# Reordering a hand-written queue: SyncE's copies of late key/query sets and first maxima, and TensorE's row blocks behind a tile preparation

## The chip, the cores and the metric

The kernel runs on one core of one Trainium2 chip. The metric is the device time of one execution in microseconds. The core has a matrix engine (TensorE, PE in the profile, with its weight loads as PEld), VectorE (DVE), ScalarE (ACT), GpSimd (POOL), and SyncE (SP), which in this kernel issues every DMA.

## The reference

A block on x of 8 sequences of 1024 tokens of 256 numbers: a layer norm, and then the sum of x, an attention with 16 query heads over 8 key/value heads and linear distance biases (ALiBi), and a linear layer with weights of 8 bits and inputs rounded to 8 bits per token.

```python
xn = _layernorm(x)
q = (xn @ Wq.T).reshape(n, s, 16, 16)
k = repeat((xn @ Wk.T).reshape(n, s, 8, 16), 2, axis=2)
v = repeat((xn @ Wv.T).reshape(n, s, 8, 16), 2, axis=2)
energy = einsum('nqhd,nkhd->nhqk', q, k) - abs(t_q - t_k) * slope_h
attn = softmax(energy / 4, axis=-1)
attention = einsum('nhqk,nkhd->nqhd', attn, v).reshape(n, s, 256) @ Wo.T + bo
x_scale = maximum(max(abs(xn), axis=-1), 1e-6) / 127
x_q = clip(round(xn / x_scale), -128, 127)
linear = (x_q @ weight_q.T) * x_scale * weight_scale + bias
out = x + attention + linear
```

## The kernel before

The work is 64 **units**, one for each batch and key/value head (u = 8 * batch + head), each with two query heads (e = 0, 1), and 64 **tiles** of 128 tokens. Each engine runs its own list of instructions, written out by hand; semaphores tie the lists together. Nothing is reordered at run time, so an instruction that waits holds up all behind it on its engine.

**A unit on PE** (`unit` under `pe`, L1417) has eight slots, c = 0 to 7, one for each block of 128 keys. A slot holds four column products (`col_half`, L1279: scores of a key block against 512 queries of one head, into a ring of three PSUM banks), two row blocks (`ahead_row_block`), and one product with V (`pv_block`, L1355). The column products give the scores that ACT turns into probabilities (L1171). The **row blocks** are scores of 128 queries against all 1024 keys, computed one or two units ahead: row blocks 0 to 7 of unit u are those of unit u + 1, head 1, and 8 to 15 those of unit u + 2, head 0. DVE finds the maximum of each row (L999, "reduction" below). Two PSUM buffers, `ps_row`, take turns, so row block i waits for the reduction of row block i - 2. The maxima go back into the query rows as two extra rows, so that the column products come out less their maximum.

**A row block** comes in two shapes. `half_row_block` (L1296 and L1298) runs two products side by side in the two halves of PE's rows; its second half reads a copy of keys and queries on other partitions, `k_again` and `q_again`. `row_block` (L1279 into `ps_row`) runs eight products in strips of 32 columns and needs no copy.

**Preparation of tiles.** In the odd units 1 to 53, at the end of slot c = 1, PE makes queries, keys, values and the linear layer of one or two tiles (`outputs`, `qkv_whole`, L1395 to L1415) and, from unit 9 on, the output projection of earlier tiles. DVE has its share of that at the same place: normalisation and statistics (L915 to L957), and before them the transposition of the last unit's sums (L1039). A "pair" below is an odd unit from this place on and the even one behind it, up to the next odd unit's preparation.

**SP's list** (`unit` under `sp`, L597) issues, for each unit, the next x tile, the transposed x tile (`load_xt`), the set of keys and queries of unit u + 3 (`next_set`, some 12 DMAs), stores of attention sums and of prepared parts, the token scales (`load_token`, L568), the maxima of unit u + 1 into its query rows (`place_max`, L506, four small DMAs), the attention rows to project (L525), the copy `k_again`/`q_again` of unit u + 3 (`load_again`, L497 and L499) and the outputs. The first column product of a unit waits for its maxima (`set_loaded` up to `WHOLE_SET`).

A set is **late** (`late_set`) when the last tile of its batch is prepared in the very unit that should load it: units 8, 16, ... 56, seven in all. Such a set is loaded at the end of unit u - 3, and its `load_again` comes in unit u - 2, at the end of that unit's list. PE runs the late unit's head 0 as strips, without the copy, in unit u - 2, and its head 1 with the copy from slot 0 of unit u - 1 on (`wait_again`). `load_again(u)` itself waits until the set has landed and until the row blocks of unit u - 2 are done, since the two copies take turns. The change of unit 22 to unit 23 (late set 24) stands for the seven below.

Before the first unit, SP stores the first tiles' parts, loads sets 0 to 2 and the remaining constants, and ends with the first `load_token`, two `load_again` and `place_max(0, 0)`.

Of the kernel before, what the change touches and what calls it, by code (L numbers as in the profile page):

```python
# [41 lines left out]
UNITS = BATCH * KV_HEADS  # L42
# [42 lines left out]
SETS = 4  # L85
# [19 lines left out]
def last_tile(u):  # L105

    return BLOCKS * (u // KV_HEADS + 1) - 1


def late_set(u):  # L110

    return u >= SETS - 1 and last_tile(u) >= PREP_AHEAD and made_unit(last_tile(u)) == u - SETS + 1
# [77 lines left out]
def build(nc, x, x_t, wqk_t, wv_t, wo_t, wo_last_t, w8_t, w_scale, bias_attn, bias_lin, q_alibi, k_alibi, diag,  # L190
          eye, parts_dram, token_dram, att_dram, out):
    ctx = ExitStack()
    with ctx:
# [237 lines left out]
        def _(sp):  # L431
# [20 lines left out]
            def load_set(u, slot):  # L452

                g, tok = u % KV_HEADS, (u // KV_HEADS) * SEQ

                def rows(dst, chunk, row, pick, loaded=set_loaded[slot]):
                    for at, q_parts, k_parts in PAIRS:
                        use = q_parts if pick == "q" else k_parts
                        n = len(use)
                        cols = bass.ds(chunk * TOKENS + tok, SEQ)  # L460
                        here = dst[at:at + n * HEAD_DIM, :]
                        if len(set(use)) == 1:
                            src = parts_dram[bass.ds(row, HEAD_DIM), use[0]:use[0] + 1, cols]
                            sp.dma_start(here, src.rearrange("d j n -> j d n").broadcast_to(  # L464
                                [n, HEAD_DIM, SEQ])).then_inc(loaded, 16)
                        elif list(use) == sorted(use):
                            src = parts_dram[bass.ds(row, HEAD_DIM), use[0]:use[0] + n, cols]
                            sp.dma_start(here, src.rearrange("d j n -> j d n")).then_inc(loaded, 16)
                        else:
                            for j, part in enumerate(use):  # L470
                                src = parts_dram[bass.ds(row, HEAD_DIM), part:part + 1, cols]
                                sp.dma_start(here[j * HEAD_DIM:(j + 1) * HEAD_DIM, :],
                                             src.rearrange("d j n -> (d j) n")).then_inc(loaded, 16)

                pairs = KV_HEADS // (QK_CHUNKS - 1)
                rows(k_set[:, slot, :], QK_CHUNKS - 1, g * HEAD_DIM, "k",
                     first_rows_loaded if u == 0 else set_loaded[slot])
                for e in range(GROUP):
                    rows(q_set[:, slot, e, :], g // pairs, (g % pairs * GROUP + e) * HEAD_DIM, "q",
                         first_rows_loaded if u == 0 and e == 0 else set_loaded[slot])  # L480
                if u >= SETS - 1:
                    load_alibi(u, slot)
# [75 lines left out]
            def store_token(t):  # L558
                sp.wait_ge(xscale_ready, 3 * (t - PREP_AHEAD + 1))
                sp.dma_start(token_dram[t, :, :],  # L560
                             token_of(t)).then_inc(token_stored[t % 2], 16)

            def load_token(t):

                sp.wait_ge(token_stored[t % 2], stored_tokens(t))
                if t >= PREP_AHEAD + 2:
                    sp.wait_ge(xt_scaled, t - 2 - PREP_AHEAD + 1)
                sp.dma_start(token_b[:, t % 2, :, :].rearrange("p n j -> p (n j)"),  # L568
                             token_dram[t:t + 1, :, :].rearrange("a n j -> a (n j)").broadcast_to(
                                 [P, TOKEN * P])).then_inc(token_loaded[t % 2], 16)  # L570
# [15 lines left out]
            for dst, src in ((wscale, w_scale), (bias, bias_attn), (bias2, bias_lin)):  # L586
                sp.dma_start(dst[:, :], src.unsqueeze(0).broadcast_to([P, EMBED])).then_inc(
                    consts_loaded, 16)
            load_set(2, 2)
            sp.dma_start(wo[:, :, :], wo_t.rearrange("(c p) n -> p c n", p=P)).then_inc(  # L590
                consts_loaded, 16)
            sp.dma_start(wo_last[:, :, :], wo_last_t).then_inc(wo_last_loaded, 16)
            for t in (PREP_AHEAD, PREP_AHEAD + 1):
                load_xt(t)
            store_token(PREP_AHEAD)
            load_token(PREP_AHEAD)
            load_again(1, 1)  # L597
            load_again(2, 2)
            place_max(0, 0)

            def unit(u, f):
                if f["next_x"]:
                    next_x(u + X_AHEAD)
                if f["xt"]:
                    load_xt(u + 2 + PREP_AHEAD)
                if f["row_set"] and not late_set(u + 3):
                    next_set(u + 3)
                if u % PAIR == 1:
                    store_att(u - 1)
                for t in f["normed"]:  # L610
                    store_token(t)
                for t in f["made"]:
                    store_parts(t, t % 2)
                if u == UNITS - 3:
                    load_att_last(0, P, UNITS - KV_HEADS // EC)
                if f["last"]:
                    load_att_last(1, P - GROUP * HEAD_DIM, UNITS - 1)
                if f["token"]:
                    load_token(u + 1 + PREP_AHEAD)
                if not f["last"]:  # L620
                    place_max(u + 1, (u + 1) % SETS)
                if f["prev"] and u % PAIR == 0:
                    store_att(u - 1)
                for t in f["next_att"]:
                    load_att_t(t, t % 2)
                if f["row_set"]:
                    if late_set(u + 3):
                        next_set(u + 3)
                    else:
                        load_again(u + 3, (u + 3) % SETS)  # L630
                if u + 2 < UNITS and late_set(u + 2):
                    load_again(u + 2, (u + 2) % SETS)
                for t in finished(u):
                    store_out(t, t % 2)

# [580 lines left out]
        def _(pe):  # L1216
# [202 lines left out]
            def unit(u, f):  # L1419
                for c in range(BLOCKS):  # L1420
                    if c == 0:
                        pe.wait_ge(set_loaded[u % SETS], set_count(u, u % SETS, WHOLE_SET))
                    col_half(u, c, 0, 0)
                    col_half(u, c, 0, 1)
                    ahead_row_block(u, f, 2 * c)
                    ahead_row_block(u, f, 2 * c + 1)
                    col_half(u, c, 1, 0)
                    if c >= 2:
                        pv_block(u, u % 2, c - 2)
                    elif f["prev"]:  # L1430
                        pv_block(u - 1, (u - 1) % 2, BLOCKS - 2 + c)
                    col_half(u, c, 1, 1)
                    if c == 1:
                        for t in f["proj"] or f["made"]:
                            outputs(u, f, t % PAIR)
                        for t in f["made"]:
                            qkv_whole(u, t)
# [52 lines left out]
```

## Time and profile before

| what | value |
|---|---|
| median of 3 runs | 1608.16 us (1606.62 to 1609.25) |
| profiled execution, own time | 1606.43 us |
| its span, first to last instruction | 1604.5 us |
| PE busy | 1507.3 us, 94% of the span |
| DVE busy | 1394.1 us, 87% |
| ACT busy | 1183.8 us, 74% |
| POOL busy | 1073.4 us, 67% |
| mean granted TensorE clock | 0.978 |

The profile is one execution. "Busy" is time in which an engine has at least one instruction in flight. In the timeline, times count from the first instruction; a row can merge several instructions of one kind (x8), and a bracket at its end gives the idle time ahead of it and what ended that. Matmuls overlap: a row of eight column products starts eight matmuls, and the next row may start before the last has drained. The list of waits sums, for each pair of a waiting line and what it waited for, the idle time, how often, and the longest.

### The profile page before, as it was taken

What the parts mean: (1) busy time and instruction counts of PE and PEld (TensorE: products, weight loads), DVE (VectorE), ACT (ScalarE), POOL (GpSimd) and SP (SyncE); (2) the same over time, 40 slices, a digit from 0 to 9 for tenths busy, and PEclk for the clock granted to TensorE, in tenths of its full rate; (3) what the DMA queues carried; (4) which work ended last, traced back from release to release, by engine and by line L of the source; (5) the groups of instructions that cost most, each with busy time, mean ns of one, the idle gap of its engine ahead of it and who ended that gap; (6) DMA issues with size and microseconds to landing.
All of it is one profiled execution on the core that took longest, in us unless ns stands there. A gap on an engine that the chain in (4) does not pass through costs nothing.

```text
span 1604.5 us, 42517 instructions
## 1 busy us (share of the span) xinstructions
PE 1507.3 (94%) x16284; PEld 584.2 (36%) x16284; DVE 1394.1 (87%) x1698; ACT 1183.8 (74%) x2331; POOL 1073.4 (67%) x1627
## 2 busy tenths in 40 slices
PE   5789989999899998999989999899998999899999
PEld 5323323333333333333333334333333333233333
DVE  6889989999799997999979999799987988899991
ACT  3467777777687775887757887677776777688885
POOL 6457877777688875787757787577785776433332
PEclk9899999999999999999999999999999999999999
DMA  6423233343324333333333333333333332212211
GB/s 169 130 62 84 71 99 79 89 98 84 105 72 106 96 79 98 93 93 101 84 84 95 103 90 90 89 94 97 94 86 85 95 85 69 80 44 70 70 42 61
DMA packets 197291, 140.98 MB, mean 88 GB/s; under 512 B 107040, under 2 KB 165728, under 8 KB 197088
## 3 DMA queue, kind: packets, MB, share of 16 engines
q1 hardware_dynamic: 197088, 138.27, 33.0%
q8 instruction: 129, 2.11, 0.6%
q14 instruction: 74, 0.61, 0.1%
HBM read 81.40 MB, written 35.63 MB: 73 GB/s over the span
## 4 chain that ended last, share of the span: by engine, by line
PE 53%; DVE 31%; issue 8%; SPq 4%; DMA 3%; POOL 0%; ACT 0%; POOLq 0%; ACTq 0%
DVE row_max L999 29%; PE ps_ring L1279 17%; PE ps_pv L1355 15%; PE ps_row L1296 11%; PE ps_ring L1395 4%; PE ps_ring L1415 3%; DMA q_again<-q 2%; PE ps_ring L1398 1%; DVE pv_turned L1039 1%; PE ps_row L1279 1%; PE ps_ring L1409 1%; SPq L497 1%; PE ps_row L1387 1%; SPq L464 0%; DMA base<-x 0%
## 5 line engine op out<-in xcount | busy, mean ns | idle before, releaser
L999 DVE TENSOR_REDUCE row_max<-ps_row 128x1 f32<-128x1024 f32 x1024 | 1199.2, 1213 | 153.8 <-PE ps_row L1298 138.5
L1171 ACT ACTIVATE probs<-ps_ring 128x512 f32<-128x512 f32 x2048 | 1083.7, 601 | 284.8 <-PE ps_ring L1279 282.3
L1279 PE MATMUL ps_ring<-q,k 122*32 122x512 bf16 x8192 | 639.2, 385 | 5.6 <-DMA q<-neg_max_t 4.7
L762 POOL TENSOR_TENSOR probs<-probs,near 128x256 f32<-128x256 f32 x512 | 374.2, 731 | 368.5 <-ACT probs L1171 362.8
L1355 PE MATMUL ps_pv<-probs,v_unit 128*32 128x512 f32 x4096 | 537.9, 601 | 0.0
L1279 PEld LDWEIGHTS ps_ring<-q,k 122*32 122x32 bf16 x8192 | 216.5, 95 | 511.7 <-ACT probs L1171 324.6
L1296 PE MATMUL ps_row<-k,q 64*128 64x512 bf16 x944 | 329.7, 390 | 68.1 <-DMA q_again<-q 43.2
L1298 PE MATMUL ps_row<-k_again,q_again 64*128 64x512 bf16 x944 | 329.6, 390 | 0.0
L1296 PEld LDWEIGHTS ps_row<-k,q 64*128 64x128 bf16 x944 | 83.9, 93 | 362.9 <-issue 197.8
L1355 PEld LDWEIGHTS ps_pv<-probs,v_unit 128*32 128x32 f32 x4096 | 125.2, 110 | 55.1 <-issue 9.1
L1298 PEld LDWEIGHTS ps_row<-k_again,q_again 64*128 64x128 bf16 x944 | 83.8, 93 | 0.0
L817 POOL CAST parts<-qk 128x384 bf16<-128x384 f32 x53 | 26.6, 502 | 83.4 <-ACT qk L1180 83.4
L1395 PE MATMUL ps_ring<-xn_t,wqk 128*128 128x128 f32 x636 | 79.9, 275 | 0.5 <-ACT probs L1171 0.5
L1395 PEld LDWEIGHTS ps_ring<-xn_t,wqk 128*128 128x128 f32 x636 | 77.0, 192 | 2.5 <-ACT probs L1171 1.3
L1039 DVE STREAM_TRANSPOSE pv_turned<-ps_pv 128x512 f32<-128x512 f32 x64 | 45.2, 706 | 28.4 <-PE ps_pv L1355 28.4
L809 POOL TENSOR_SCALAR xq_t<-xround 128x256 bf16<-128x256 f32 x53 | 57.3, 1081 | 4.5
L801 POOL TENSOR_SCALAR xround<-xt_step 128x256 f32<-128x256 f32 x53 | 57.0, 1075 | 4.5
L689 POOL TENSOR_TENSOR parts<-rest,parts 128x384 bf16<-128x384 f32 x59 | 54.1, 917 | 7.2 <-ACT parts L1127 3.0
L1177 ACT ACTIVATE v_all<-ps_ring 128x128 f32<-128x128 f32 x53 | 14.7, 277 | 58.5 <-PE ps_ring L1398 58.5
L1415 PE MATMUL ps_ring<-wo,att_t 128*128 128x256 f32 x224 | 57.4, 382 | 0.0
L1279 PE MATMUL ps_row<-k,q 120*32 120x512 bf16 x640 | 45.3, 390 | 11.7 <-issue 8.9
L819 POOL TENSOR_TENSOR rest<-qk,parts 128x384 f32<-128x384 f32 x53 | 48.5, 916 | 4.3
(84 smaller groups left out, 1009.1 us busy)
## 6 DMA issues: line engine op xcount, KB each, us to landing
parts_dram<-parts SPq DMA_DIRECT2D x59, 288.0 KB, 3.3
q_again<-q SPq DMA_DIRECT2D x63, 256.0 KB, 3.4
token_b<-token_dram SPq DMA_DIRECT2D x53, 256.0 KB, 4.0
q<-parts_dram SPq DMA_DIRECT2D x128, 96.0 KB
k<-parts_dram SPq DMA_DIRECT2D x256, 32.0 KB
q<-parts_dram SPq DMA_DIRECT2D x128, 64.0 KB
att_dram<-att_unit SPq DMA_DIRECT2D x126, 64.0 KB
att_t<-att_dram SPq DMA_DIRECT2D x56, 128.0 KB, 2.9
```

Source lines behind the costliest of these rows:

```text
L762: pool.tensor_tensor(here, here, near[:, u % KV_HEADS, :].rearrange("p (e n) -> p e n", e=GROUP), ALU.mult).then_inc(weighted, 1)
L801: pool.tensor_scalar(xround[:, :], xt_step[:, 1, :, :].rearrange("p c n -> p (c n)"), Q_MAX, ROUND, ALU.min, ALU.add).then_inc(xt_rounded, 1)
L809: pool.tensor_scalar(xq_t[:, t % TURNED, :, :].rearrange("p c n -> p (c n)"), xround[:, :], -ROUND, -Q_MAX - 1, ALU.add, ALU.max).then_inc ...
L999: dve.tensor_reduce(row_max[:, par, e, qb:qb + 1], ps_row[qb % 2][:, :], AX_X, ALU.max, negate=True).then_inc(row_max_found, 1)
L1039: dve.transpose(pv_turned[:, :], ps_pv[:, :]).then_inc(pv_read, 1)
L1171: act.activation(probs[:, c % PBUFS, e, h * HALF:(h + 1) * HALF], ring_bank(u, c, e, h), ACT.Exp, scale=SCALE).then_inc(ring_freed, 1)
L1279: mm = pe.matmul(to[at, :], weights[:, at], moving, start=start, stop=stop)
L1296: pe.matmul(ps_row[qb % 2][:, 0:HALF], q_set[0:ROW_K, slot, e, at], k_set[0:ROW_K, slot, 0:HALF], start=True, stop=True)
L1298: pe.matmul(ps_row[qb % 2][:, HALF:SEQ], q_again[ROW_K:2 * ROW_K, u % AGAIN, e, at], k_again[ROW_K:2 * ROW_K, u % AGAIN, :], start=True, s ...
L1355: mm = pe.matmul(ps_pv[32 * j:32 * j + 32, :], v_unit[:, par, c, :], probs[:, c % PBUFS, j // 2, (j % 2) * HALF:(j % 2 + 1) * HALF], start ...
L1395: pe.matmul(bank[:, m * P:(m + 1) * P], wqk[:, c, m * P:(m + 1) * P], xn_t[:, t % TURNED, c, :], start=(c == 0), stop=(c == EC - 1))
L1415: mm = pe.matmul(bank[:, EMBED:2 * EMBED], att_t[:, t % 2, c, :], wo[:, c, :], start=(c == 0), stop=(c == EC - 1))
```

## The change

Three edits, none of which adds or removes an instruction. Ahead of the first unit, SP's `load_again(1, 1)` moves ahead of the output weights, and `place_max(0, 0)` ahead of `load_again(2, 2)` and the first `load_token`. In SP's unit, `load_again` of a late set moves from near the end of the list to right behind `load_xt`, ahead of `next_set`. In PE's unit, where tiles were prepared in slot 1 (`f["made"]`), the two row blocks of slot 2 come ahead of that slot's first two column products.

```diff
             load_set(2, 2)
+            load_again(1, 1)
             sp.dma_start(wo[:, :, :], wo_t.rearrange("(c p) n -> p c n", p=P)).then_inc(
                 consts_loaded, 16)
             sp.dma_start(wo_last[:, :, :], wo_last_t).then_inc(wo_last_loaded, 16)
             for t in (PREP_AHEAD, PREP_AHEAD + 1):
                 load_xt(t)
             store_token(PREP_AHEAD)
+            place_max(0, 0)
+            load_again(2, 2)
             load_token(PREP_AHEAD)
-            load_again(1, 1)
-            load_again(2, 2)
-            place_max(0, 0)
...
                 if f["xt"]:
                     load_xt(u + 2 + PREP_AHEAD)
+                if u + 2 < UNITS and late_set(u + 2):
+                    load_again(u + 2, (u + 2) % SETS)
                 if f["row_set"] and not late_set(u + 3):
                     next_set(u + 3)
...
                     else:
                         load_again(u + 3, (u + 3) % SETS)
-                if u + 2 < UNITS and late_set(u + 2):
-                    load_again(u + 2, (u + 2) % SETS)
                 for t in finished(u):
                     store_out(t, t % 2)
...
-                    col_half(u, c, 0, 0)
-                    col_half(u, c, 0, 1)
+                    behind_tiles = c == 2 and f["made"]
+                    if not behind_tiles:
+                        col_half(u, c, 0, 0)
+                        col_half(u, c, 0, 1)
                     ahead_row_block(u, f, 2 * c)
                     ahead_row_block(u, f, 2 * c + 1)
+                    if behind_tiles:
+                        col_half(u, c, 0, 0)
+                        col_half(u, c, 0, 1)
                     col_half(u, c, 1, 0)
```

SP's list ahead of the first unit, as a difference; L590 and L592 are the output weights, L560 and L568 the token scales' store and load, L506 the first maxima (the line numbers shift by one behind the first added line):

```order
-L590 DMA wo<-wo_t 128x2x256
-L592 DMA wo_last<-wo_last_t 128x1024
+L497 DMA k_again<-k 64x512
+L499 DMA q_again<-q 64x2048
+L591 DMA wo<-wo_t 128x2x256
+L593 DMA wo_last<-wo_last_t 128x1024
 L555 DMA xt<-x_t 128x2x128 x2
 L560 DMA token_dram<-token 128x4
-L568 DMA token_b<-token_dram 128x512
-L497 DMA k_again<-k 64x512
-L499 DMA q_again<-q 64x2048
-L497 DMA k_again<-k 64x512
```

The maxima stood last of this stretch, behind both copies and the token load, whose load waits for the store one row above it; now the copy of unit 1 goes out first, and the maxima follow the token store directly.

SP's list in unit 6, the first of the seven with a late set (8), before; L468 is the first DMA of the set of unit 9, and the second pair of L497 and L499 is the late set's copy:

```order
L488 DMA k<-k_alibi 10x1024
L568 DMA token_b<-token_dram 128x512
L506 DMA q<-neg_max_t 2x16x32 x4
L516 DMA att_dram<-att_unit 4x16x256 x2
L497 DMA k_again<-k 64x512
L499 DMA q_again<-q 64x2048
L497 DMA k_again<-k 64x512
L499 DMA q_again<-q 64x2048
L433 DMA base<-x 128x256
```

The same unit's head, now:

```order
L433 DMA base<-x 128x256
L555 DMA xt<-x_t 128x2x128
L497 DMA k_again<-k 64x512
L499 DMA q_again<-q 64x2048
L468 DMA k<-parts_dram 32x1x1024
L464 DMA k<-parts_dram 16x1024
L472 DMA k<-parts_dram 16x1024 x3
```

The late copy has moved past the whole next set, the token load, the maxima, the attention store and the other copy; all of these now stand behind it.

PE in an odd unit behind a preparation, as a difference; L1398 is its last product, L1279 into `ps_ring` are column products (four matmuls each), L1296 and L1298 row blocks:

```order
 L1398 MATMUL ps_ring<-wv,xn_t 128x128 x2
-L1279 MATMUL ps_ring<-q,k 32x512 x8
-L1296 MATMUL ps_row<-k,q 128x512
-L1298 MATMUL ps_row<-k_again,q_again 128x512
-L1296 MATMUL ps_row<-k,q 128x512
-L1298 MATMUL ps_row<-k_again,q_again 128x512
-L1279 MATMUL ps_ring<-q,k 32x512 x4
+L1296 MATMUL ps_row<-k,q 128x512
+L1298 MATMUL ps_row<-k_again,q_again 128x512
+L1296 MATMUL ps_row<-k,q 128x512
+L1298 MATMUL ps_row<-k_again,q_again 128x512
+L1279 MATMUL ps_ring<-q,k 32x512 x12
```

Two column products stood between the preparation and the row blocks; now all three of head 0's two halves and head 1's first half follow the row blocks in one piece.

## Rows read from the trace of the kernel before

**Rows 1.** The page, chain that ended last: share of the span by engine

```profile
PE 53%; DVE 31%; issue 8%; SPq 4%; DMA 3%; POOL 0%; ACT 0%; POOLq 0%; ACTq 0%
```

**Rows 2.** Waits, whole span: engine line waited for, us in total, times, longest

```profile
PEld ps_row L1296 <- DVE row_max L999: 98.7, 260, 2.4
...
PE ps_row L1296 <- DMA q_again<-q: 43.2, 7, 7.2
...
PE ps_ring L1279 <- DMA q<-neg_max_t: 4.7, 1, 4.7
```

**Rows 3.** Timeline, PE, end of unit 22 and start of unit 23: start, us, what

```profile
608.27 1.04 PE L1279 MATMUL ps_row<-k,q 120*32 120x512 bf16 x16
...
618.10 0.82 PE L1279 MATMUL ps_ring<-q,k 122*32 122x512 bf16 x12
625.91 0.60 PE L1296 MATMUL ps_row<-k,q 64*128 64x512 bf16 x1 [6.99 <-DMA q_again<-q]
...
630.11 0.39 PE L1296 MATMUL ps_row<-k,q 64*128 64x512 bf16 x1
```

**Rows 4.** Timeline, SP, unit 22: sets 24 and 25, maxima of 23, late copy

```profile
601.00 0.70 SPq L468 DMA_DIRECT2D q<-parts_dram  x1
...
604.19 0.62 SPq L468 DMA_DIRECT2D k<-parts_dram  x1
...
612.23 2.67 SPq L506 DMA_DIRECT2D q<-neg_max_t  x4
...
622.09 0.59 SPq L499 DMA_DIRECT2D q_again<-q  x1
```

**Rows 5.** Chain that ended last, first reductions behind three preparations (units 19, 21, 23)

```profile
537.29 2.37 DVE row_max L999 x2
...
583.54 2.37 DVE row_max L999 x2
...
638.88 2.37 DVE row_max L999 x2
```

**Rows 6.** Timeline, SP, PE and DVE, ahead of and in unit 0

```profile
32.69 0.73 SPq L468 DMA_DIRECT2D q<-parts_dram  x1
...
37.20 1.90 PE L1279 MATMUL ps_row<-k,q 120*32 120x512 bf16 x16 [8.91 <-issue]
...
58.71 0.47 SPq L560 DMA_DIRECT2D token_dram<-token  x1
...
67.72 3.17 SPq L506 DMA_DIRECT2D q<-neg_max_t  x4
...
72.12 1.04 PE L1279 MATMUL ps_ring<-q,k 122*32 122x512 bf16 x8 [4.74 <-DMA q<-neg_max_t]
...
59.48 9.17 DVE L999 TENSOR_REDUCE row_max<-ps_row 128x1 f32<-128x1024 f32 x8
...
73.74 2.36 DVE L999 TENSOR_REDUCE row_max<-ps_row 128x1 f32<-128x1024 f32 x2 [5.10 <-PE ps_row L1298]
```

**Rows 7.** Timeline, PE, DVE and ACT behind unit 19's preparation; DVE in unit 18

```profile
536.31 0.62 PE L1279 MATMUL ps_ring<-q,k 122*32 122x512 bf16 x8
536.86 0.39 PE L1296 MATMUL ps_row<-k,q 64*128 64x512 bf16 x1
...
539.24 0.39 PE L1296 MATMUL ps_row<-k,q 64*128 64x512 bf16 x1
...
541.87 0.39 PE L1296 MATMUL ps_row<-k,q 64*128 64x512 bf16 x1
...
537.29 3.60 DVE L999 TENSOR_REDUCE row_max<-ps_row 128x1 f32<-128x1024 f32 x3 [0.54 <-PE ps_row L1298]
...
536.96 1.58 ACT L1171 ACTIVATE probs<-ps_ring 128x512 f32<-128x512 f32 x3
538.93 2.15 ACT L1171 ACTIVATE probs<-ps_ring 128x512 f32<-128x512 f32 x4 [0.38 <-PE ps_ring L1279]
...
510.72 0.70 DVE L1039 STREAM_TRANSPOSE pv_turned<-ps_pv 128x512 f32<-128x512 f32 x1
```

## Prediction

> **What bounds the kernel now.** I read the chain that ended last first: half of the span goes over PE and nearly a third over DVE's reductions [rows 1], so the two engines drive each other, and work on ACT, POOL or SP counts only where one of these two waits for it. The list of waits then says where they do [rows 2]. Three items matter: 260 short waits of PE's weight loads for reductions, seven long ones of PE for the copy q_again (43.2 us), and one of 4.7 us for the first maxima. The timeline shows where these stand: the seven at the head of units 7, 15, ... 55 [rows 3], the single one ahead of unit 0 [rows 6], the short ones in about every second slot [rows 7]. The three edits aim at these three places, one each.
>
> **The late copy (seven places).** In unit 23, PE has done two column products and then stands still for 6.99 us until 625.91 [rows 3], because SP issued that copy last, at 622.09 [rows 4]. The seven stalls sum to 43.2 us [rows 2].
>
> The stall costs more than itself. The first slot after it lasts from 625.91 to 630.11, 4.20 us [rows 3]; an ordinary slot without a wait goes from 536.86 to 539.24, 2.38 us [rows 7]. The difference, 1.82 us, is a PE at half clock after it stood still. Seven times 1.82 is 12.7 us. As a cross-check, from unit 21's first reduction behind its preparation to unit 23's are 55.34 us, from unit 19's to unit 21's 46.25 [rows 5]: 9.09 us more, of which 6.99 and 1.82 are these two, and 0.3 is left for the strips of the late set, which stay. What goes if no wait takes its place: 43.2 + 12.7 = 55.9 us.
>
> Now the copy is issued at the head of unit 22, where SP must wait for set 24 to land. No row shows that landing. The nearest is the first set: its last query DMA was issued at 32.69, and PE, which needs it, began at 37.20 [rows 6], 4.5 us later. Set 24's last query DMA was issued at 601.00 [rows 4], so I take 605.5. At the latest it landed at 608.27, when PE used it [rows 3].
>
> Behind this wait stand, on SP, the whole next set, the token load and the maxima of unit 23. A pair of copies takes 1.2 us of SP's time (the last one 0.59 [rows 4], the first about as much). So the next set begins at about 606.8 instead of 604.19, 2.6 us later, and the four maxima DMAs, 612.23 to 614.90 [rows 4], end at 617.5. The first maxima landed 1.23 us after their last issue (70.89 to 72.12 [rows 6]); these would at 618.7. PE's first column product of unit 23 is the second of the three that start at 618.10 [rows 3], due at 618.3. So PE waits about 0.4 us there. Seven times that is 2.8 us. The ends are nothing (landing half a microsecond sooner) and 3.2 us each (landing at 608.27). I keep 0.4, since the 4.5 us include PE's own reaction and the DMA queue is emptier when SP pauses. The copy itself lands well before PE asks. The attention rows, behind the maxima on SP, also slip by about as much as the unit's head does, and their user stands two slots into unit 23.
>
> Sum: 55.9 - 2.8 = 53.1 us less.
>
> **The first maxima.** PE stops at 67.38 and starts unit 0 at 72.12, 4.74 us later, when the maxima issued from 67.72 to 70.89 have landed [rows 6]. They are ready long before: the eight reductions that follow their transposition on DVE begin at 59.48 [rows 6]. SP is held up by the token load, which waits for the token store issued at 58.71. In the new list the token store ends at 59.18 + 1.2 for the copy that was put ahead = 60.4, the maxima are issued by 63.6, and land by 64.8, or 2 us later if the bytes of the weights ahead of them hold them up. Either is before 67.38. The token load waits as before, and its reader on POOL comes behind a weighting in unit 0. Next late is DVE: its reductions run until 68.65 [rows 6], so its wait of 5.10 us ahead of the reduction at 73.74 goes, and that is the gain, 5.1 us. If the half clock after this stall also goes without a replacement, up to 1.8 more, by the price above; if the maxima land late, 3.
>
> **Row blocks ahead of column products (27 places, 23 of them with projections).** PE's work is the same. Before, the column products start at 536.31 and row block 4 at 536.86, its reduction at 537.29 after DVE idled 0.54 [rows 7]. Now row block 4 takes 536.31 and the reduction 0.55 earlier, at about 536.75. What that buys: slots alternate between 2.38 us (536.86 to 539.24) and 2.63 (539.24 to 541.87), the 0.25 being the second row block's wait for the reduction two blocks earlier [rows 7]. With the reductions 0.55 earlier slot 3 has no wait. But its own first reduction starts when row block 6 is done, at the same 539.24 as before, and slot 4, now 0.25 earlier, must wait 0.25 for it. So the wait moves from slots 3, 5, 7 to 4, 6, 0, and every second slot ends where it did. In slot 1 of the even unit DVE has its transposition of 0.70 us (510.72 [rows 7]), behind which DVE alone sets the next start, at the same time in both orders. Gain: 0.
>
> Against that, ACT gets the first column product 0.55 us later. It takes 1.58 us for the three before the fourth, which it awaits for 0.38 us [rows 7]; the three would end at about 538.9 (536.86, one matmul of 0.4, then 1.58), just when PE asks for the third bank again. Cost 0 to 0.15 us, 23 times: at most 3.5 us. In units 1 to 7, without projections, PE's share is shorter and DVE comes last, so nothing changes.
>
> One switch between matmul shapes fewer remains. From the first of two column products to the row block are 0.55 us [rows 7], and two column products take 0.22 each (three start within 0.82 less the 0.39 of the last [rows 3]), so 0.11 goes with the switch; ACT's delay can take it back. The Trainium skill (TensorEngine Tiling (Array Packing), Key Properties) says that changing the tiling mode drains the engine; the new order has two such changes behind a preparation where the old had three, which would leave the gain of rival 3, 1546.5 in place of 1549.
>
> **The sum.** 1606.4 (own time of the profiled execution) - 53.1 - 5.1 - 0 = 1548.2. The median of the runs lies 1.7 us above the profiled execution; halfway between, I say **1549 us**.
>
> **Rivals.**
> 1. *The maxima become the wait.* The set lands as late as rows allow, 608.27, and each unit head loses 3.2 us instead of 0.4: 7 x 2.8 = 20, so 1569; with a half clock after it, 12.7 more, 1581. For: SP is one list, and everything behind the copy waits with it. Against: 4.5 us in the nearest row, and no wait of PE at 608.27.
> 2. *The row blocks pay.* If one short wait falls out in each pair instead of moving (DVE's transposition not absorbing it), 23 x 0.25 = 5.8 us: 1543.
> 3. *The fewer switches pay.* ACT's delay costs nothing and 0.11 us stays in each of 23 pairs, 2.5 us: 1546.5. The Trainium skill's rule on drains, above, points here.
> 4. *The first maxima don't come sooner*, since over a megabyte stands ahead of them in the queue: 5.1 us back, 1554.
> 5. *Slower.* SP's stand at the head of unit 22 delays the maxima of unit 23 so much that it outweighs everything: it decides from 58/7 = 8.3 us more per late set, a set landing after 616. At 10 us: 1549 + 70 = 1619. Against: PE itself used the set at 608.27.
>
> **How the numbers follow.** Forecast 0.64; rival 1 0.12; rival 2 0.10; rival 3 0.06; rival 4 0.06; rival 5 0.02. The low end of the range takes in rival 2 together with a microsecond or two of half clock in unit 0, 1541. The high end takes in rival 4 and half of rival 1, 1564. The rest of rival 1 and rival 5 stay outside, and some mixed cases. A measurement tells 0.2%, some 3 us, from no change; all but rival 5 lie far on the faster side: faster 0.97, same 0.01, slower 0.02.
>
> **What would show it.** Right: no row of PE waiting for q_again; the pair across a late set lasts about 47 us between the reductions of [rows 5]; at the heads of units 7 to 55 a wait for the maxima of below 1 us; unit 0 starts at 67.4; the granted clock stays full at all eight places; ordinary pairs stay at 46.25 with the waited slots shifted by one. Wrong: PE waiting for q<-neg_max_t for 3 us or more (rival 1), ordinary pairs of 46.0 (rival 2), a new wait of ACT or of the column products behind a preparation that makes them longer than 46.4.

## The result: 1569.5 us, and the profile after

| | before | after |
|---|---|---|
| median (4 runs each) | 1607.83 us | **1569.53 us** (1568.87 to 1574.19) |
| ratio, 95% interval | | 0.9768 (0.9747 to 0.9789) |
| profiled execution | 1606.43 us | 1568.87 us |
| PE's waits for q_again | 43.2 us, 7 times | none |
| PE's waits for the maxima | 4.7 us, once | 16.8 us, 8 times |

The kernel is 2.3% faster, but 20 us of the forecast gain are missing: 1569.5 against 1549, and outside 1541 to 1564. It is rival 1's time, 1569, to within a microsecond. Two runs at a lower granted clock, one of the late copy alone (1664.66 us) and one of the kernel before (1651.24 us), are in no median and no ratio below.

The waits of the changed kernel (engine line waited for: us in total, times, longest), to be read against [rows 2]:

```profile
PEld ps_ring L1279 <- ACT probs L1171: 356.0, 1193, 0.8
...
PEld ps_row L1296 <- DVE row_max L999: 104.8, 284, 2.1
...
PE ps_ring L1279 <- DMA q<-neg_max_t: 16.8, 8, 3.8
```

The stall on the copy has gone from the list, and the maxima have taken part of its place. The chain that ended last, shares of the span, against [rows 1]:

```profile
PE 49%; DVE 27%; SPq 9%; issue 9%; DMA 3%; POOL 3%; ACT 0%; POOLq 0%; DVEq 0%
```

SP's issuing has gone from 4% to 9%: SP's list now sets the end in stretches ahead of the late units. PE's timeline at the first column product of units 0, 7, 23 and 31 (start, us, what, idle time before it and what ended it):

```profile
68.77 0.61 PE L1279 MATMUL ps_ring<-q,k 122*32 122x512 bf16 x8 [0.28 <-DMA q<-neg_max_t]
231.66 1.04 PE L1279 MATMUL ps_ring<-q,k 122*32 122x512 bf16 x8 [2.75 <-DMA q<-neg_max_t]
610.85 0.61 PE L1279 MATMUL ps_ring<-q,k 122*32 122x512 bf16 x8 [2.11 <-DMA q<-neg_max_t]
800.57 0.62 PE L1279 MATMUL ps_ring<-q,k 122*32 122x512 bf16 x8 [3.77 <-DMA q<-neg_max_t]
```

Unit 0's wait is the first of the four. All seven late boundaries have such a wait: 2.75, 3.47, 2.11, 3.77, 1.68, 1.94 and 0.77 us, 16.5 in all, 2.36 on average where 0.4 was forecast. SP's timeline in unit 22 shows how it comes about (compare [rows 4]):

```profile
591.01 0.70 SPq L468 DMA_DIRECT2D q<-parts_dram  x1
591.75 0.83 SPq L488 DMA_DIRECT2D k<-k_alibi  x2
...
593.50 0.46 SPq L555 DMA_DIRECT2D xt<-x_t  x1
596.58 0.56 SPq L497 DMA_DIRECT2D k_again<-k  x1
597.18 0.59 SPq L499 DMA_DIRECT2D q_again<-q  x1
598.01 0.66 SPq L468 DMA_DIRECT2D k<-parts_dram  x1
...
605.40 0.35 SPq L568 DMA_DIRECT2D token_b<-token_dram  x1
605.80 2.70 SPq L506 DMA_DIRECT2D q<-neg_max_t  x4
```

SP is free at 593.96 and issues the copy at 596.58: it stands 2.62 us for set 24. From there to the maxima it never pauses; they are the last four of 20 DMAs that follow one another without a stop. The chain says the same, as pieces in order of time:

```profile
592.23 4.33 DMA k<-k_alibi
...
607.88 2.92 DMA q<-neg_max_t
...
610.85 0.61 PE ps_ring L1279 x8
```

The set's last DMA lands and releases SP; the last of the maxima lands and releases PE. It was issued until 608.50 and landed at 610.80, 2.30 us later. PE was ready at 608.74.

Half clock came back after three of the seven waits. Windows of PE (from and to, length in us, busy us and matmuls, granted clock, share of the DMA engines, GB/s), at unit 7's head and then at unit 23's:

```profile
232.00:233.00 1.00, 1.00 (x10) 0.50 0.62 172
233.00:234.00 1.00, 1.00 (x11) 0.50 0.98 201
...
611.00:612.00 1.00, 1.00 (x16) 1.00 0.93 252
612.00:613.00 1.00, 1.00 (x12) 1.00 0.65 180
```

Behind 2.75 us of standing the granted clock is 0.50 of full, that is 1.2 GHz instead of 2.4; behind 2.11 us it is full.

### The profile page after: what moved, and what is told of

Read it like the earlier page. It is cut to its first block, busy times and chain, and to the rows that moved or that the text cites. A ratio compares the mean times of both kernels' runs of the same rounds, so it can differ in the third digit from the quotient of the medians.

```text
span 1566.9 us, 42517 instructions
## 1 busy us (share of the span) xinstructions
PE 1499.6 (96%) x16284; PEld 583.0 (37%) x16284; DVE 1397.0 (89%) x1698; ACT 1185.3 (76%) x2331; POOL 1076.2 (69%) x1627
## 3 DMA queue, kind: packets, MB, share of 16 engines
q8 instruction: 129, 2.11, 0.6%
## 4 chain that ended last, share of the span: by engine, by line
PE 49%; DVE 27%; SPq 9%; issue 9%; DMA 3%; POOL 3%; ACT 0%; POOLq 0%; DVEq 0%
DVE row_max L999 24%; PE ps_ring L1279 15%; PE ps_pv L1355 13%; PE ps_row L1296 10%; PE ps_ring L1395 4%; PE ps_ring L1415 3%; SPq L464 2%; DMA k<-k_alibi 2%; SPq L506 2%; SPq L468 2%; SPq L472 1%; PE ps_ring L1398 1%; DMA q<-neg_max_t 1%; DVE pv_turned L1039 1%; PE ps_ring L1409 1%
## 5 line engine op out<-in xcount | busy, mean ns | idle before, releaser
L1279 PE MATMUL ps_ring<-q,k 122*32 122x512 bf16 x8192 | 636.5, 383 | 18.2 <-DMA q<-neg_max_t 16.8
L1279 PEld LDWEIGHTS ps_ring<-q,k 122*32 122x32 bf16 x8192 | 214.4, 95 | 532.6 <-ACT probs L1171 356.0
L1296 PE MATMUL ps_row<-k,q 64*128 64x512 bf16 x944 | 326.6, 386 | 25.6 <-DVE row_max L999 11.0
L1298 PE MATMUL ps_row<-k_again,q_again 64*128 64x512 bf16 x944 | 326.5, 385 | 0.0
L1296 PEld LDWEIGHTS ps_row<-k,q 64*128 64x128 bf16 x944 | 82.5, 93 | 303.9 <-issue 178.8
L1298 PEld LDWEIGHTS ps_row<-k_again,q_again 64*128 64x128 bf16 x944 | 82.3, 93 | 0.0
L1279 PE MATMUL ps_row<-k,q 120*32 120x512 bf16 x640 | 45.6, 392 | 12.0 <-issue 9.2
```

The costliest lines, as they stand in the source:

```text
L1279: mm = pe.matmul(to[at, :], weights[:, at], moving, start=start, stop=stop)
L1296: pe.matmul(ps_row[qb % 2][:, 0:HALF], q_set[0:ROW_K, slot, e, at], k_set[0:ROW_K, slot, 0:HALF], start=True, stop=True)
L1298: pe.matmul(ps_row[qb % 2][:, HALF:SEQ], q_again[ROW_K:2 * ROW_K, u % AGAIN, e, at], k_again[ROW_K:2 * ROW_K, u % AGAIN, :], start=True, s ...
```

## The experiments

Every ratio is to runs of the kernel before on the same chip, taken beside those of the kernel named. Two kernels from different rows are best compared by these ratios. "Seven" is the sum of PE's waits for the maxima at the seven late unit heads in the profiled execution.

| kernel | median, us | ratio (95%) | what PE waited for |
|---|---|---|---|
| first maxima alone | 1602.80 | 0.9975 (0.9962 to 0.9989) | q_again 42.9; maxima of unit 0 2.2 |
| late copy alone | 1575.32 | 0.9790 (0.9768 to 0.9812) | seven 16.1; unit 0 5.1 |
| row blocks alone | 1609.95 | 1.0014 (1.0004 to 1.0023) | q_again 44.5; unit 0 4.6 |
| late copy behind the next set | 1549.88 | 0.9646 (0.9633 to 0.9658) | maxima 4.0 in all |
| the same, no row edit | 1548.27 | 0.9634 (0.9617 to 0.9651) | maxima 3.1 in all |
| late copy behind the maxima, no row edit | 1547.09 | 0.9626 (0.9609 to 0.9643) | maxima of unit 0 1.5; q_again 0.3 |
| next set behind the maxima | 1581.57 | 0.9843 (0.9821 to 0.9866) | attention rows 20.5; maxima of unit 0 1.9, of unit 8 4.9 |
| maxima ahead of the token load | 1562.14 | 0.9720 (0.9698 to 0.9743) | seven 15.1; unit 0 1.9 |
| late sets' alibi rows earlier | 1562.13 | 0.9716 (0.9693 to 0.9739) | seven 12.9; unit 0 2.0 |
| changed kernel, no row edit | 1569.52 | 0.9766 (0.9748 to 0.9783) | seven 17.1; unit 0 1.5 |
| changed kernel again | 1568.24 | 0.9758 (0.9739 to 0.9777) | seven 18.9; unit 0 0.3 |
| late copy behind the maxima, last weights later | **1544.89** | **0.9612** (0.9596 to 0.9628) | q_again 1.7 |

**The three edits apart.** Each kernel has one of the edits of the diff and the other two places as before.

> The edit of SP's list ahead of the first unit alone. Theory (the three edits add up, and this one is worth the move of unit 0's reductions in the trace of after, 5.8 us): about 1602 us, a wait of PE for the first maxima below 0.5 us, the other seven waits of 4.6 to 7.2 us for q_again as before. Rival (part of the 5.8 us belongs to another start of the execution, not to the edit): 1603 to 1605 us.

> The late copy at the head of SP's unit alone. Theory (SP's list holds up the next maxima): about 1575 us, 33 us less than before; seven waits of PE for q<-neg_max_t that sum to about 16 us, none for q_again but the one wait of 4.7 us ahead of unit 0 stays. Rival (the three edits lean on each other): anything outside 1572 to 1578 us.

> The row blocks ahead of the column products alone. Theory (the short wait only moves by a slot, and the later column products cost some 0.08 us a pair): 1 to 2 us more than before, pairs of 46.33 us against 46.25. Rival (a short wait falls out of each pair): 5 us less, pairs of 46.0 us.

Measured: 0.25% faster, 2.1% faster, 0.14% slower. The ratios multiply to 0.978 (0.9975 x 0.9790 x 1.0014 = 0.9779), and the whole change has 0.9768: within the intervals the edits add up, and the shortfall is in the late copy. The wait for the maxima stands there when that edit is alone:

```profile
PE ps_ring L1279 <- DMA q<-neg_max_t: 21.2, 8, 5.1
```

5.1 of it is unit 0, which this kernel leaves as it was; 16.1 is the same seven waits.

**The place of the copy in the list.** If it is SP's standing that delays the maxima, the same copy thirteen DMAs later in the same unit, when the set has long landed, costs no standing and still comes long before PE needs it.

```diff
-                if u + 2 < UNITS and late_set(u + 2):
-                    load_again(u + 2, (u + 2) % SETS)
                 if f["row_set"] and not late_set(u + 3):
                     next_set(u + 3)
...
+                if u + 2 < UNITS and late_set(u + 2):
+                    load_again(u + 2, (u + 2) % SETS)
                 if f["token"]:
                     load_token(u + 1 + PREP_AHEAD)
```

> After, with the late copy issued behind the next set (ahead of the token load and the maxima) instead of ahead of it. Theory of the list (SP's stand of some 2.6 us for the landing set is what makes the maxima late; here the set has long landed): no stand of SP, the maxima 1.2 us later than in before and in time, waits for q<-neg_max_t below 0.5 us each and none for q_again: about 1549 us. Rival (the 320 KB of the copy stand ahead of the maxima in the DMA queues and hold them up): the copy is now nearer to the maxima, so waits of 2 to 4 us stay at all seven places: 1565 to 1575 us.

1549.88 us, against the forecast's 1549 for the changed kernel itself. SP's timeline in unit 22 of this kernel:

```profile
591.67 0.84 SPq L488 DMA_DIRECT2D k<-k_alibi  x2
592.61 0.56 SPq L497 DMA_DIRECT2D k_again<-k  x1
593.22 0.59 SPq L499 DMA_DIRECT2D q_again<-q  x1
593.91 0.54 SPq L568 DMA_DIRECT2D token_b<-token_dram  x1
594.49 2.74 SPq L506 DMA_DIRECT2D q<-neg_max_t  x4
```

The copy follows the set's last row without a gap, and the maxima go out right behind. What is left of the wait, as this kernel's list of waits has it:

```profile
PE ps_ring L1279 <- DMA q<-neg_max_t: 4.0, 5, 1.1
```

No row of PE waits for q_again. The 320 KB of the copy are now nearer to the maxima, and the wait is smaller, so the rival of this experiment is out. That settles the mechanism: the copy had only to leave the end of the list, and the head is one place too far.

Two more kernels take the row edit out, and one of them puts the copy behind `place_max`:

> Late copy behind the next set as in behind_set, the prologue's edit, and PE's order as in before. Theory (the row blocks ahead of the column products cost some 2 us, as rows_only showed): 1.5 to 2.5 us less than behind_set, about 1547.5 us; pairs of 46.25 us. Rival (the cost is only there beside the long waits): 1549 to 1551 us.

> The same with the late copy one place later, behind the token load and the maxima of the next unit. Theory of the list (each instruction of SP delays only what stands behind it): the maxima are as early as in before, so no wait for q<-neg_max_t in units 7 to 55; the copy is issued some 4 us later than in behind_set_no_rows and lands at about the time PE asks, with waits for q_again of 0 to 1 us each; about 1546 to 1550 us. Rival (the copy lands too late): waits for q_again of 1.5 us and more each, above 1556 us.

1548.27 and 1547.09 us. With the copy behind the maxima PE's only wait for maxima is the first one, 1.5 us ahead of unit 0. The weight loads wait for the copy by a little (2.5 us, 5 times, of which PE itself loses 0.3), so it is now about as late as it may be. The difference between the two kernels is within their intervals.

**The next set out of the way.** Here the copy stays at the head, and in those seven units the set behind it goes after the maxima:

```diff
-                if f["row_set"] and not late_set(u + 3):
+                if f["row_set"] and not late_set(u + 3) and not late_set(u + 2):
                     next_set(u + 3)
...
                 if not f["last"]:
                     place_max(u + 1, (u + 1) % SETS)
+                if f["row_set"] and late_set(u + 2):
+                    next_set(u + 3)
```

> Late copy at the head of SP's unit as in after, but in those seven units the next set behind the maxima; PE's order as in before. Theory of the list: the stand of SP for the landing set stays (2.6 us at the unit's head) but no longer reaches the maxima, which are issued as soon as DVE has them: no waits for q<-neg_max_t. What stands behind the set, the attention rows for unit u + 1's projection, comes some 5 us later than in after and makes PE wait at the end of its slot 1, by 1 to 4 us each: 1550 to 1575 us. Rival (the stand itself or the early copy costs): waits for q<-neg_max_t of 2 us and more stay.

1581.57 us. The waits for maxima at the seven heads are gone, as the list theory has it, and the time is still 12 us longer than that of the changed kernel, for another reason. The list of waits (lines are two higher here; L1417 is the output projection):

```profile
PE ps_ring L1417 <- DMA att_t<-att_dram: 20.5, 6, 3.8
```

The set, some 7 us of SP's time, now stands ahead of the attention rows, whose user is two slots into the next unit. At six of the seven places PE waits for them instead, and the clock halves after five. At the seventh, unit 7 has no projection; there the maxima of unit 8 came late on the same list, and PE stood 4.91 us at the head of unit 8, with half clock behind it. The forecast had a sentence on these rows and gave them no price, since they slipped as much as the unit's head.

**What delays the maxima's landing.** From the end of the last issue to PE's start are 1.6 to 2.5 us at the seven heads, against 1.23 in [rows 6]. (The 2.2 to 3 us in the text below count from the start of the last issue, the 1.2 from its end; like for like, the difference is smaller.) Directly ahead of them stands the token load, 256 KB.

```diff
-                if f["token"]:
-                    load_token(u + 1 + PREP_AHEAD)
                 if not f["last"]:
                     place_max(u + 1, (u + 1) % SETS)
+                if f["token"]:
+                    load_token(u + 1 + PREP_AHEAD)
```

> After, with the maxima issued ahead of the token load in every unit. Theory (the 256 KB of the token load, issued 0.4 us ahead of the maxima, also hold up their landing, 2.2 to 3 us behind the last issue instead of 1.2): the maxima are issued 0.4 us sooner and land 1.2 to 1.7 us behind their last issue, so the seven waits fall from 16.5 us to 6 to 9 us in all: about 1558 to 1562 us. Rival (the landing time has another cause): the waits fall by the 0.4 us of the issue alone, to some 13.5 us, about 1566 us.

From the end of the last issue to PE's start still were 1.7 to 2.6 us, so the token load isn't the cause. The time is 1562.14 us; the profiled execution has 15.1 us of seven, only 1.4 less than the changed kernel's, and is itself the longest of this kernel's (1566.6). That explains a part of the 6 to 7 us; the rest stays open.

**What the set's landing hangs on.** Behind the last query DMA of a set come two small ones, the alibi rows (L488). This kernel issues those of a late set earlier, in the time in which SP stands for POOL:

```diff
                 for t in f["normed"]:
                     store_token(t)
+                if f["row_set"] and late_set(u + 3):
+                    if u + 3 >= SETS:
+                        wait_filled(sp, u + 3 - SETS, BLOCKS - 1, GROUP - 1, 1)
+                    load_alibi(u + 3, (u + 3) % SETS)
                 for t in f["made"]:
                     store_parts(t, t % 2)
```

> The changed kernel, with one difference: the two alibi rows of a late set are loaded before the stores of prepared parts in the unit in which that set is loaded, where SyncE stands for GpSimd anyway, so that a query DMA is the last of the set. Theory (the set lands some 4.0 to 4.5 us after whatever DMA is issued last, and the forecast had counted from the last query DMA although two alibi DMAs follow it): in unit 22 SyncE's copy of the late set goes out about 0.9 us sooner against the set's first DMA, 10.1 us after it instead of 11.1, the maxima land as much sooner, and PE's waits for them at the seven unit heads fall from 16.6 us to about 10, 0.9 us less each, with one or two of the three half-clock stretches gone: about 1560 us, 1557 to 1564. Rival (the set's bytes set the landing, not the last issue): the copy goes out 11 us after the set's first DMA as before, the waits stay at 15 to 17 us, 1567 to 1571.

SP's timeline in unit 22 of it:

```profile
583.78 0.62 SPq L468 DMA_DIRECT2D k<-parts_dram  x1
...
589.30 0.69 SPq L468 DMA_DIRECT2D q<-parts_dram  x1
...
594.57 0.56 SPq L497 DMA_DIRECT2D k_again<-k  x1
```

From the set's first DMA to the copy are 10.79 us here, 11.07 in the changed kernel (585.51 to 596.58). Over the seven places the means are 11.03 and 11.36: 0.33 sooner, where 0.9 was expected and the rival had 0. From the end of the last issue the copy now takes 4.73 us on average, 4.14 in the changed kernel. The 0.33 is no more than the places differ among themselves (10.53 to 11.68 here, 11.07 to 11.87 in the changed kernel), and the changed kernel's second profile has a mean of 11.30. So the theory doesn't hold: the query rows alone land at nearly the same time, and the alibi rows add a third of a microsecond at most. The time, 1562.13, lies where the theory put it, but the mechanism it names carries only part of that: seven is 12.9 us, 3.6 less than in the changed kernel's first profile and 6.0 less than in its second, and the clock still halves after three of the seven heads. What the rest of the gain comes from stays open.

**The row edit, and the kernel's own spread.**

> The changed kernel without its third edit: column products stand ahead of the row blocks behind a preparation, as in the kernel before. If the row edit costs what it did alone and behind the other two edits in the earlier runs, 1.5 to 2.3 us, this takes about 1567.5 us (ratio 0.9755). Rival, the row edit costs nothing here because PE's waits for the maxima take it up: 1569.5 (ratio 0.9768). The waits for maxima at the seven unit heads stay at 15 to 18 us in either case.

> The changed kernel once more, on the same chip and beside the same runs of the kernel before as the other three of this call: 1569.5 us (1568 to 1574), ratio 0.9768, and waits for the maxima of 16 to 18 us. It settles whether the 1562 us of the variant with the maxima ahead of the token load lies outside the spread of this kernel.

1569.52 and 1568.24 us: beside the waits for maxima the row edit can't be told from nothing, since the intervals are as wide as the 2 us in question. The changed kernel's second profile has 18.9 us of seven, its first 16.5, with half clock after four of the heads instead of three. Single waits differ by up to 1.5 us between the two profiles (2.11 and 3.65 at unit 23's head).

**The best of it.** `wo_last`, 512 KB that nobody reads until the last unit, goes behind the first token load:

```diff
-            sp.dma_start(wo_last[:, :, :], wo_last_t).then_inc(wo_last_loaded, 16)
             for t in (PREP_AHEAD, PREP_AHEAD + 1):
                 load_xt(t)
             store_token(PREP_AHEAD)
             place_max(0, 0)
             load_again(2, 2)
             load_token(PREP_AHEAD)
+            sp.dma_start(wo_last[:, :, :], wo_last_t).then_inc(wo_last_loaded, 16)
```

> The fastest order so far (late copy behind the maxima, no row edit, 1547.1 us), and the last output weights, 512 KB that are needed only after the last unit, loaded behind the first token load instead of ahead of the first maxima. If the bytes of weights ahead of the first maxima are what makes these land 4.7 to 5.4 us after their last issue, they land 1 to 3 us sooner, the wait of 1.5 us ahead of unit 0 goes, and the time is about 1545.5 us (ratio 0.9616). Rival, the bytes of the weights do not matter: the wait stays at 1.5 us and the time at 1547.

1544.89 us, 3.9% less than before and 1.5% less than the changed kernel beside the same runs of before (0.9612 / 0.9758). SP and PE ahead of unit 0:

```profile
59.78 2.77 SPq L506 DMA_DIRECT2D q<-neg_max_t  x4
...
66.31 0.62 PE L1279 MATMUL ps_ring<-q,k 122*32 122x512 bf16 x8
```

There is no bracket behind PE's row: the first maxima, issued until 62.55, are there before PE is. With the weights ahead of them, in the kernel with the copy behind the maxima, PE stood 1.51 us:

```profile
60.44 4.11 SPq L506 DMA_DIRECT2D q<-neg_max_t  x4
...
68.61 0.63 PE L1279 MATMUL ps_ring<-q,k 122*32 122x512 bf16 x8 [1.51 <-DMA q<-neg_max_t]
```

There the four took 4.11 us to issue, until 64.55, and PE began 4.06 us after that. Without the 512 KB ahead of them they took 2.77 us to issue, and had landed 3.76 us after that at the latest (62.55 to 66.31). In all ten profiles with the new list and these weights ahead, PE began 4.0 to 4.25 us after the last issue and had stood for 0.3 to 2.25 us. So the weights count. How much of the landing is theirs isn't shown, since 3.76 us is only an upper bound; and by time alone the two kernels can't be told apart, as their intervals overlap. What is left in this kernel are two waits of PE for the late copy, 0.84 and 0.89 us.

## Why the prediction missed, step by step

**The late copy, removed cost: right.** The 43.2 us of stalls and the half clock behind them are gone. (The prediction took the 1.82 us for half clock without a row; a window of PE in unit 23 of the kernel before has the granted clock of 0.50.)

```profile
628.00:629.00 1.00, 1.00 (x12) 0.50 0.24 74
```

Where nothing takes their place, they are worth what was said, within the interval. The kernel with the copy behind the maxima and the row edit left out is 60.1 us below its runs of before (0.0374 x 1607.58); the forecast for these two edits was 55.9 + 5.1 = 61.0.

**The late copy, the new wait: the step that failed.** It was sized 0.4 us for each of seven heads, from two landings. It measured 2.36 on average, and two of the seven, 3.47 and 3.77, lie above the upper end of 3.2.

- *The set's landing*, taken as 4.5 us after its last query DMA's issue, from the first set. In unit 22 SP went on 5.57 us after it (591.01 to 596.58). So the next set slipped not by 2.6 us but by 3.8 (598.01 against about 594.2, right behind the row that ends at 593.96). The two alibi DMAs that follow the query DMA were overlooked; the experiment gives them 0.33 us of the 1.07 at most. And the row at 32.69 was misread. It is the last query DMA of the first set's head 0; three more, of head 1, follow, and PE at 37.20 needed those of head 0 alone (`first_rows_loaded` in the kernel):

```profile
34.60 0.70 SPq L468 DMA_DIRECT2D q<-parts_dram  x1
```

So the 4.5 us are the landing of eight DMAs, and a late set has thirteen. What makes up the other 0.7 isn't shown.
- *The maxima's landing*, taken as 1.23 us from the end of the last issue to PE's start, from the first maxima, measured 2.35 in unit 23 (608.50 to 610.85) and 1.6 to 2.5 at all seven, 2.0 on average. The row that it was taken from lies in a nearly empty moment. Windows of the DMA traffic (from and to, length in us, granted clock, share of the DMA engines, GB/s) in the kernel before, while the first maxima were issued and then landed:

```profile
68.00:70.00 2.00, 0.99 0.92 197
70.00:72.00 2.00, 0.50 0.08 10
```

and in the changed kernel, while those of unit 23 were issued and then landed:

```profile
606.00:608.00 2.00, 1.00 0.55 180
608.00:610.00 2.00, 1.00 0.17 50
```

While they landed the share was 0.08 there and 0.17 here, with a set of 13 DMAs and the token load just gone out; but two microseconds earlier it had been higher there, 0.92 against 0.55. So the share alone doesn't explain the difference, and which of this traffic lengthens the landing isn't settled: without the token load ahead of them it took as long, and with the set moved away there was no wait from which a landing could be read.

Over the seven heads the copy goes out 5.77 us after the set's last query DMA, 1.27 more than was taken, and the maxima take 0.77 more: 0.4 + 1.27 + 0.77 = 2.44, close to the 2.36 measured. The reason given for keeping 0.4, that the queue is emptier when SP pauses, helped neither landing: the set's took longer all the same, and the maxima go out behind 16 DMAs without a pause. The upper end, 3.2 us each, was in the text, and should have weighed more, as both terms had been borrowed from the prologue.

**Half clock.** With waits below a microsecond the clock was to stay full. With 0.8 to 3.8 us it fell after three of seven. The pairs show the price, from one preparation to the next. Rows of two reductions in the chain that ended last, each 8.4 us behind the end of a preparation (units 17, 19 and 23), to be read against the 46.25 and 55.34 us of [rows 5]:

```profile
488.51 2.37 DVE row_max L999 x2
...
534.84 2.37 DVE row_max L999 x2
...
630.26 2.37 DVE row_max L999 x2
```

From 488.51 to 534.84 is an ordinary pair, 46.33. From 534.84 to 630.26 are another of these and the late one of 49.09. That was forecast at about 47, with 0.4 us of waiting in it; here, with no half clock behind it, it has the wait of 2.11 us instead, the 0.08 of the row edit, and some 0.35 that no row names. Against the kernel before, the late pairs are 2.15, 2.23, 6.25, 3.54, 6.56 and 6.54 us shorter, and from unit 53 to the end, with the seventh place, it is 6.0 us less: 33.3 together. The three at which the clock halved are the first, second and fourth. Of the 19.8 us missing from 53.1, 13.7 are stalls (16.5 less 2.8) and some 5.5 the half clock at the old price of 1.82.

**The first maxima: right in size, by luck of one landing.** Forecast 5.1 us, measured 5.8 by a mark in unit 0 in this profile (a reduction at 81.98 that had been at 87.79), and 4.5 by the medians of the edit alone (1607.33 to 1602.80). They were to land by 64.8 or 2 us later. SP's issues ended at 64.52, not 63.6, and PE began at 68.77, 4.25 us behind them, having stood 0.28 us; in the other nine profiles with this list it stood 0.3 to 2.25 us, and half clock followed in the six of 1.5 us and more. The landing, taken as 1.23 to 3.2 us, was the term that was too small here as well. Rival 4's mechanism, the weights ahead in the queue, was real, and its price partial.

**Row blocks ahead of column products: the step right, its cost at half the upper end.** PE's weight loads in four slots behind a preparation (PEld's timeline):

```profile
529.41 0.10 PEld L1296 LDWEIGHTS ps_row<-k,q 64*128 64x128 bf16 x1
...
532.24 0.09 PEld L1296 LDWEIGHTS ps_row<-k,q 64*128 64x128 bf16 x1 [0.37 <-DVE row_max L999]
...
534.62 0.09 PEld L1296 LDWEIGHTS ps_row<-k,q 64*128 64x128 bf16 x1
...
537.25 0.09 PEld L1296 LDWEIGHTS ps_row<-k,q 64*128 64x128 bf16 x1 [0.37 <-DVE row_max L999]
```

The waited slots have moved by one, from 3, 5, 7 to 4, 6, 0, and none fell out, so rival 2 is out. ACT's delay shows in PE's timeline at the second group of column products:

```profile
526.93 0.83 PE L1279 MATMUL ps_ring<-q,k 122*32 122x512 bf16 x12
...
528.45 1.02 PE L1279 MATMUL ps_ring<-q,k 122*32 122x512 bf16 x12
```

1.02 us where the same twelve take 0.82: PE waits 0.2 us for the bank that ACT now empties later. Over the span, the weight loads of the column products wait for ACT for 356.0 us, and before for 324.6; the edit alone has 353.3, the changed kernel without it 322.2.

```profile
PEld ps_ring L1279 <- ACT probs L1171: 324.6, 1114, 0.8
```

Most of that costs nothing. An ordinary pair went from 46.25 to 46.33; 23 times 0.08 is 1.8 us, within the 0 to 3.5 stated, and the edit alone cost 0.14%, 2.3 us. Rival 3 is out too. The Trainium skill (TensorEngine Tiling (Array Packing), Key Properties) says that a change of the tiling mode drains the engine; one change less is real in the order, but no run here shows a gain from it: the wait for the bank is larger than the 0.11 us that it could be worth by the forecast.

**Rival 1** named the mechanism and the time, 1569, and got a chance of 0.12. "SP is one list, and everything behind the copy waits with it" is what happened. The argument against it, that PE used the set at 608.27 without a wait, spoke only of the latest possible landing. That its time came out to the microsecond is luck: it has the set land 7.3 us after the last query DMA, where 5.6 to 6.2 were measured, lets the maxima land as fast as forecast, and has no half clock. The 20 us that came out are 13.7 of stalls and 5.5 of half clock.

**A slip in rival 5.** 8.3 us more per late set than the forecast's 0.4 mean a set that lands at 605.5 + 8.3 = 613.8, not after 616. It changes nothing here, as the set landed long before.

## What to carry to other kernels

- A DMA that must wait for another's landing should not stand ahead of urgent ones on the same issuing engine. Put it as late as its own reader allows: the same copy at the list's end cost 43 us, at its head 16 us and three stretches of half clock, and behind the maxima 0.3 to 1.7 us.
- When a landing time is borrowed from another place of the trace, check which DMAs its reader there waited for, and look at what is queued there and what is queued here. Count both from the same end of the same DMA, the last of the whole group, and weigh the range's far end more if the place borrowed from is an idle one.
- Before judging a wait of a few microseconds on PE, ask whether half clock follows it (here 1.8 us more, after three of seven), and check who is next on the same list before moving a large group out of the way.

## What the runs showed of the hardware

- The landing of four 2 KB DMAs, from the end of the last issue to PE's start, differed by place: 1.23 us in the prologue of before, 1.1 to 2.9 us behind a set at the late heads, 4.0 to 4.25 us in the new prologue with 512 KB of weights ahead, and at most 3.76 with these behind. Full DMA engines alone don't explain it: their share was down to 0.17 while unit 23's maxima landed.
- Waits of PE of nearly one length were followed by either clock. In the kernel with the alibi rows earlier, 3.07 us at one head left the clock at full, and 1.98 at another was followed by half. In the changed kernel 2.11 was followed by full and 2.75 by half. The spread between runs of the kernel with the alibi rows earlier (1557 to 1566) is larger than that of the best one (1544.4 to 1546.0), whose longest wait for the copy is 0.89 us and which has none for maxima.
